# Evicting two neighbouring PSUM banks with one instruction, with the contracted weights kept by row tile

## The reference

```python
masked_w = weight * mask[None, :, :]
w_bot = jnp.einsum('bg,got->bot', y, masked_w)
out = x + jnp.einsum('bnt,bot->bno', x, w_bot) + bias
```

## Time and profile before

| | us |
|---|---|
| median of 3 runs | 600.57 (600.22 to 600.57) |
| span of the profiled execution, first to last instruction | 598.5 |
| TensorE matmul busy | 591.2 (99%) |
| TensorE weight load busy | 517.5 (86%) |
| VectorE busy | 318.5 (53%) |
| ScalarE busy | 138.5 (23%) |
| POOL busy | 38.0 (6%) |

### The profile page before, as it was taken

How to read it: one execution, slowest core, us unless ns; L and a number is a source line. 1 busy time by engine, 2 the same in 40 slices (tenths; PEclk the granted TensorE clock), 3 DMA queues, 4 the chain that set the end, 5 groups by cost and what they waited for, 6 DMA issues and landing times.

```text
span 598.5 us, 15121 instructions
## 1 busy us (share of the span) xinstructions
PE 591.2 (99%) x6460; PEld 517.5 (86%) x6460; DVE 318.5 (53%) x542; ACT 138.5 (23%) x278; POOL 38.0 (6%) x34
## 2 busy tenths in 40 slices
PE   7899999999999999999999999999999999999998
PEld 5899988888898888888888888888888888889887
DVE  5565445455465555555554554555555645545343
ACT  5343222122122122221221221221212212211000
POOL 3430000000000111111110000000000000000000
PEclk9999999999999999999999999999999999999999
DMA  9987556776667798998987777586775767767842
GB/s 320 406 299 221 184 179 247 230 231 245 213 220 248 254 312 274 328 334 263 319 304 243 246 228 240 207 263 207 252 225 204 278 207 229 248 213 259 298 147 88
DMA packets 62994, 148.35 MB, mean 248 GB/s; under 512 B 6976, under 2 KB 13504, under 8 KB 62928
## 3 DMA queue, kind: packets, MB, share of 16 engines
q1 hardware_dynamic: 41184, 113.00, 58.3%
q10 hardware_dynamic: 21744, 34.39, 15.4%
HBM read 113.81 MB, written 33.55 MB: 246 GB/s over the span
## 4 chain that ended last, share of the span: by engine, by line
PE 97%; DMA 1%; SPq 1%; POOL 0%; issue 0%; DVE 0%; POOLq 0%
PE ps L464 76%; PE ps L437 20%; DMA xs<-in_mask 1%; SPq L226 1%; PE ps L474 1%; SPq L232 0%; POOL wm L205 0%; PE ps L420 0%; DVE wbot L342 0%; DVE staged L375 0%; POOLq L203 0%
## 5 line engine op out<-in xcount | busy, mean ns | idle before, releaser
L464 PE MATMUL ps<-wbot,xs 128*128 128x256 f32 (+1 forms) x2272 | 456.6, 360 | 0.8 <-DVE wbot L342 0.8
L464 PEld LDWEIGHTS ps<-wbot,xs 128*128 128x128 f32 x2272 | 390.3, 190 | 51.9 <-issue 1.6
L282 ACT ACTIVATE wbot<-ps 128x512 f32<-128x512 f32 (+2 forms) x277 | 137.2, 568 | 400.6 <-PE ps L437 392.5
L370 DVE TENSOR_TENSOR staged<-ps,staged 128x512 f32<-128x512 f32 (+1 forms) x118 | 77.9, 660 | 226.6 <-PE ps L464 226.6
L342 DVE COPY wbot<-ps 128x512 f32<-128x512 f32 (+2 forms) x274 | 159.2, 644 | 10.8 <-PE ps L437 7.9
L437 PEld LDWEIGHTS ps<-y_sb,wm 32*128 32x128 f32 x4096 | 122.1, 187 | 21.3 <-issue 17.8
L437 PE MATMUL ps<-y_sb,wm 32*128 32x128 f32 x4096 | 134.5, 277 | 1.7 <-issue 1.0
L356 DVE TENSOR_TENSOR staged<-staged,bias_sb 128x512 f32<-128x512 f32 (+1 forms) x119 | 79.1, 664 | 0.0
L205 POOL TENSOR_TENSOR wm<-wm,mask_sb 128x512 f32<-128x512 f32 x16 | 20.9, 1327 | 245.4 <-DMA mask_sb<-in_mask 245.4
L370 DVE TENSOR_TENSOR staged<-ps,bias_sb 128x256 f32<-128x256 f32 (+1 forms) x24 | 12.3, 514 | 34.0 <-PE ps L464 32.3
L205 POOL TENSOR_TENSOR wm<-wm,xs 128x512 f32<-128x512 f32 x13 | 16.4, 1272 | 22.1 <-DMA xs<-in_mask 21.9
(11 more groups left out here) (4 smaller groups left out, 0.4 us busy)
## 6 DMA issues: line engine op xcount, KB each, us to landing
xs<-in_x SPq DMA_DIRECT2D x128, 512.0 KB, 4.2
out<-staged ACTq DMA_DIRECT2D x112, 256.0 KB, 4.4
staged<-in_xn SPq DMA_DIRECT2D x105, 256.0 KB, 3.7
wm<-in_w SPq DMA_DIRECT2D x12, 512.0 KB, 7.7
mask_sb<-in_mask SPq DMA_DIRECT2D x8, 512.0 KB, 7.9
out<-staged ACTq DMA_DIRECT2D x31, 128.0 KB, 3.7
wm<-in_w SPq DMA_DIRECT2D x8, 256.0 KB, 5.6
xs<-in_mask SPq DMA_DIRECT2D x4, 512.0 KB, 13.5
```

Of the source, the lines that this page charges most:

```text
L282: eng.activation(tile_place(b, j, first, end), tile_sums(b, j, first, end), ACT.Copy).then_inc(s_ev_a, 1)
L370: eng.tensor_tensor(at, by_batch(total), at if m >= OWN_X else bias_of(m), ALU.add).then_inc(s_o, 1)
L464: ins = eng.matmul(bank[:, h * width:(h + 1) * width], group[:, h, k, :], at, start=(k == 0), stop=(k == KT - 1))
```

## The change

ScalarE evicts row tiles 0 and 1 of a burst with one instruction over two neighbouring banks, and VectorE evicts tiles 2 and 3 with another, in all bursts. So that a pair lies in neighbouring banks, an even one first, `share_banks` plans the banks: a pair of a burst takes the even-aligned pair of banks whose later use is the oldest, a piece takes the single bank used longest ago; `TAKEN_FROM` says whose bank each takes, and `room` waits for that one. The 8 PSUM tensors are one tensor `ps`. The layout of `wbot` within a chunk and group was (k, h, 16 features) and is (row tile j, k, h, 4 features): a pair's values are regular in it, and a piece's moving operand, 16 features for one k and h, now lies in runs of 4 values where it had runs of 16. A burst has 2 parts, or 4 where it is cut, in `parts_of`; the test of the length of `parts_of(b)` against TILES in `group_ready` is left as it was.

```diff
-TAKEN = [(_b, _j) for _b in range(HALF) for _j in range(TILES)]
-for _m in range(LAST + 1):
-    TAKEN += [(_b, _j) for _b in bursts_before(_m) for _j in range(TILES)] + [(_m, None)]
-TAKEN += [(LAST + _i, None) for _i in range(1, len(ENDING))]
-BANK_OF = {_key: _i for _i, _key in enumerate(TAKEN)}
+BANK_OF, TAKEN_FROM = {}, {}
+def share_banks():
+    owner, given = {}, dict.fromkeys(range(BANKS), -1)
+    def take(key, bank, at):
+        BANK_OF[key], TAKEN_FROM[key], owner[bank], given[bank] = bank, owner.get(bank), key, at
+    def take_burst(b, at):
+        for p in range(2):
+            first = min(range(0, BANKS, 2), key=lambda i: (max(given[i], given[i + 1]), i))
+            for j in (0, 1):
+                take((b, 2 * p + j), first + j, at)
+    def take_piece(i, at):
+        take((i, None), min(range(BANKS), key=lambda n: (given[n], n)), at)
+    clock = 0
+    for b in range(HALF):
+        take_burst(b, clock := clock + 1)
+    for m in range(LAST + 1):
+        for b in bursts_before(m):
+            take_burst(b, clock := clock + 1)
+        take_piece(m, clock := clock + 1)
...
-def on_vector(b, j):
-    return j == 3 or j == 1 and b not in BY_VECTOR[:2]
+def on_vector(b, p):
+    return p == 1
...
 def parts_of(b):
     if b == HALF - 2:
-        return tuple((b, j, 0, SOON if j else GROUPS) for j in range(TILES))
+        return tuple((b, p, 0, SOON if p else GROUPS) for p in range(2))
     if b == HALF - 1:
-        return (tuple((b, j, 0, SOON) for j in range(TILES)) +
-                tuple((b - 1, j, SOON, GROUPS) for j in range(1, TILES)) +
-                tuple((b, j, SOON, GROUPS) for j in range(TILES)))
+        return (tuple((b, p, 0, SOON) for p in range(2)) + ((b - 1, 1, SOON, GROUPS),) +
+                tuple((b, p, SOON, GROUPS) for p in range(2)))
     if b % CS < CS - 1:
-        return tuple((b, j, 0, GROUPS) for j in range(TILES))
-    return tuple((b, j, at, end) for at, end in ((0, SOON), (SOON, GROUPS)) for j in range(TILES))
+        return tuple((b, p, 0, GROUPS) for p in range(2))
+    return tuple((b, p, at, end) for at, end in ((0, SOON), (SOON, GROUPS)) for p in range(2))
...
-        sums = wbot[:, :].rearrange("p (i q k h o) -> p i q k h o", i=CS, q=GROUPS, k=KT, h=GB)
+        sums = wbot[:, :].rearrange("p (i q j k h o) -> p i q j k h o", i=CS, q=GROUPS, j=TILES, k=KT, h=GB)
...
-        def tile_ready(eng, b, j):
-            eng.wait_ge(s_s1, b * TILES + j + 1)
+        def pair_ready(eng, b, p):
+            eng.wait_ge(s_s1, b * TILES + 2 * p + 2)
...
+        def pair_place(b, p, first, end):
+            at = sums[:, first:end, c, 2 * p:2 * p + 2, :, :, :] if u % 2 else sums[:, c, first:end, 2 * p:2 * p + 2, :, :, :]
+            return at.rearrange("p g j k h o -> p (j k h) g o")
+        def pair_sums(b, p, first, end):
+            at = BANK_OF[b, 2 * p] * BANK
+            return psum[:, at:at + 2 * BANK].rearrange("p (a g o) -> p a g o", g=GROUPS, o=TO)[:, :, first:end, :]
         def tile_evicted(eng, b, j, end):
-            eng.wait_ge(s_ev_v if on_vector(b, j) else s_ev_a, DONE[b, j, end])
+            p = j // 2
+            eng.wait_ge(s_ev_v if on_vector(b, p) else s_ev_a, DONE[b, p, end])
...
                 if g in (0, SOON):
                     b = u * CS + end - 1
                     soon = g == 0 and len(parts_of(b)) > TILES
-                    for j in range(TILES):
+                    for j in (0, 2):
                         tile_evicted(eng, b, j, SOON if soon else GROUPS)
...
-                        at = sums[:, g, c:end, k, h, :] if u % 2 else sums[:, c:end, g, k, h, :]
+                        at = sums[:, g, c:end, :, k, h, :] if u % 2 else sums[:, c:end, g, :, k, h, :]
```

## The result

The changed kernel takes 641.71 us (639.45 to 643.01, 4 runs) against 600.57 (600.22 to 600.82, 4 runs): the ratio is 1.068, 95% interval 1.066 to 1.070. Forecast was 635.2, with a range of 628 to 648. Run once more beside the experiments it took 641.01 us.

The account below looks back on a forecast made before the run. TensorE, without slack, bounds the kernel and would wait for later-freed banks: 22.1 + 6.6 + 1.4 + 2.0 + 2.5 = 34.6 us, on a 598.5 us span 633.1, plus 2.07 gives 635.2 us; range 628 to 648.

Parts of the forecast that it names:

- From an eviction's end to TensorE: Delay from ScalarE's eviction ending to the waiting weights' load beginning, read from the start of the trace: 0.05 us.
- Regular places: Steady part, 34 places where the piece waits for VectorE's pair behind the bias addition: 0.65 us each, 22.1 us.
- Places without the bias: 13 places where VectorE has no or a short bias addition before the copy: 0.51 us each, 6.6 us.
- The three early ones: Three early places where matmuls with the identity lengthen burst B: 0.47 us each, 1.4 us.
- ScalarE's places: 8 places where the piece takes the bank of ScalarE's pair: 0.25 us each, 2.0 us.
- POOL beside L356: Two places where POOL's mask multiplications lengthen add_bias_to_x, delaying VectorE's copy: 2.5 us, by phase 0 to 4.
- The start: Bursts 2 to 7 and the first piece: later-freed banks against fewer instructions, set to zero, -0.8 to +0.5 us.
- The wait for all of burst 15: Unit's second half piece waits for the whole last burst: hidden by the stall ahead, otherwise 0.1 us, 8 times.
- Cover holds: Rival: VectorE's pair ends within 0.57 us, no piece waits, 599.4 to 600.6 us; 3% faster, 4% same, together.
- The pair at 1.37: Rival: VectorE's pair instruction is no cheaper than two copies, 1.37 us; loss 43.8 us, time 644; 7%.
- Reading slower: Rival: TensorE reads its moving operand in runs of 4 slower: up to 14 us on top, 650; 6%.
- The clock: Rival: PE's idling drops its clock to 1.2 GHz for each piece m: over 800 us; 1%.

Follow-up runs that it names:

- the first tile alone and the test mended: Changed kernel, pieces on ScalarE's bank, ScalarE evicting tiles 0 and 1 of burst A by an instruction each, `group_ready` test mended to `len(pairs_of(b)) > 2`: 600.48 us, ratio 1.000.
- The kernel with the bias behind: Changed kernel with add_bias_to_x of the coming piece issued behind VectorE's evictions and not ahead of them: 637.16 us, ratio 1.061.
- the one with the test mended: Changed kernel with only the `group_ready` test mended, so a unit's second half piece waits for the last burst's first three groups alone: 641.04 us, beside 641.01 unmended.
- the kernel where the piece is on time: Changed kernel, pieces on ScalarE's bank by a planner key, ScalarE evicting tiles 0 and 1 of burst A by an instruction each, test unmended: 602.32 us, ratio 1.003.

## Why the prediction was right, and where its sizes were off

**The mechanism was right.** PE has no slack, the first bank after two bursts had a margin of 0.22 us, and the change takes it away. The waits confirm it, and so does each kernel that moves the moment at which the awaited bank comes free. The margin itself was read too wide: with the 0.11 us from an eviction's end to the weights' load (below), about 0.11 of the 0.22 us was slack, an estimate.

In a regular place, us after the bursts' start, and the kernel's time:

| the piece waits for | bank free | piece starts | time |
|---|---|---|---|
| ScalarE's first tile | 1.79 | 2.01 | 600.5 |
| VectorE's first tile (8 places on ScalarE's pair) | 2.07 | 2.21 | 613.6 |
| ScalarE's pair | 2.26 | 2.40 | 622.6 |
| ScalarE's second tile (52 places) | 2.27 | 2.42 | 620.3 |
| VectorE's pair (8 places on ScalarE's pair) | 2.60 | 2.74 | 641.7 |

The number of instructions plays no part: of the kernels with row 1's time, the one with the first tile alone and the test mended has 406 on VectorE, as many as the kernel of the last row.

**The sum, 34.6 us, measured 40.7 in the profiled execution** from the first pair of bursts to the end. By its terms, from the starts of bursts in the trace:

- Pair's duration, 1.217 and 1.023 us: measured 1.217 and 1.024 (from the earlier trace rows). Two banks in one instruction cost what the line through 96 and 512 elements says, and the bounds of 1.15 and 1.37 fall away.
- From an eviction's end to TensorE, 0.05 us: this was the term taken too small. 444.52 + 1.22 = 445.74, the weights' load begins at 445.85: 0.11 us. The row that I took it from the earlier trace rows was that of a row tile's load in the start, and not of a whole array's after row tiles; whether that makes the difference wasn't tried. The matmul then starts 0.03 after its load; that part comes back, as the 32 records of the two pieces take 0.03 less. So 0.06 us in each of 60 places, 3.6 us.
- Regular places: 0.65 forecast, 0.71 measured (9.82 - 9.11).
- Places without the bias: 0.51 forecast, 0.65 measured. Beside the 0.06, the copy started 1.32 us after the bursts and not 1.24: the wait for all four tiles instead of two, which the text left out. I had looked at the spread of the last four matmuls, 0.02 us, and not at that of their signals. 13 places, 1.1 us; ScalarE's part of it is 0.04 in 8 places. The three early ones are 0.61 for 0.47, likewise.
- ScalarE's places: 0.25 forecast, 0.37 measured in 7, none at m = 2, where burst 9 waits for its mask; 2.6 us for 2.0.
- POOL beside L356: 2.5 us forecast in two places, 1.2 of it above two ordinary waits; in the profiled execution three places are 0.64, 0.64 and 0.81 us above their like, 2.1 us. The kernel with the bias behind shows it: 641.4 - 637.2 = 4.2 us gone, of which 36 x 0.06 = 2.2 is the earlier copy, and most of the spread between runs with it. The forecast that this is a matter of phase, 0 to 4 us, holds: in the changed kernel's second trace (span 637.2) one place is 0.16 us above its like, in the one with the test mended (span 640.3) four are, by 2.9 us together. With the clock in the start (below), that is nearly all of the spread.

These differences, from unrounded starts, add up: 2.2 us in the 36 places with the bias, 1.9 in the 13 without, 0.4 in the early three, 0.6 in ScalarE's and 0.9 by POOL are 6.0, and 34.6 + 6.0 = 40.6. All five have the same sign; that the range held them is in part luck, since its upper end had 9 us for a dearer pair, which did not come.

**The start**, set to zero: in the profiled execution the first pair of bursts after the first piece begins 2.0 us later than before (24.93 for 22.91). In the kernels with pairs whose clock stayed at 1.00 it is between -0.1 and 0.6 (the forecast said -0.8 to 0.5), and the rest is the clock, below. The two runs that the median lies between have a mean clock of 1.000, so the 41.1 us between the medians hold no such part.

**Edits costed at nothing.** The layout: 600.34, right, by the kernel that has it alone. Banks of the bursts: the waits show none of L460 for L394; right. The wait for all of burst 15: hidden behind the late piece, as written (641.04 beside 641.01), and in the kernel where the piece is on time 1.8 us, where the text said 0.8: 0.17 in place of 0.1 us at the starts of 7 units and 0.13 before piece 8 is 1.3, and the remaining 0.5 us I can't place.

**Rivals.** Cover holds: decided at 0.57 us, the copy takes 1.217. The pair at 1.37: no. Reading slower: no. The clock: not in the steady part, 1.00 in each window of it, but see below. The change does what it says.

## What to carry to other kernels

When the bound engine runs without a gap, look for who frees its next buffer and by how much it is early; here 0.22 us in 600, at one place of a period, and it was all the kernel had. Merging two instructions saves their fixed part on an engine that may not need it, and holds the first half's buffer until the second is done: merge where nobody waits for the first half, which in this kernel was three of four pairs, and even there it gave nothing, since the engines that it relieved had slack. A planner that breaks ties by a buffer's number should break them by who is done first; in the kernel with pairs that line alone was worth 19 us.

## What the runs showed of the hardware

**Signals of row tiles come one after another.** The last matmuls of four row tiles end within 0.02 us, but an engine that waits for the first, second, third and fourth signal starts its eviction 1.19, 1.23, 1.28 and 1.32 us after the bursts' start: 0.043 us each. With signals on row tiles 1 and 3 alone the starts are 1.207 and 1.267. Both sets fit 0.025 us for each signal waited for and 0.017 for each row tile, an estimate from these six starts; so about 0.02 us between neighbours stays however few signals are raised.

**A clock that fell in the start in some executions and not in others.** In the profiled execution of the changed kernel PE waited 1.46 us for POOL's mask, and the granted clock was then 0.50, that is 1.2 GHz, for 3.4 us (its timeline, and its window in the columns of the earlier trace rows):

```profile
16.60 1.68 PE L460 MATMUL ps<-y_sb,wm 32*128 32x128 f32 x29 [1.46 <-POOL wm L229]
```

```profile
16.88:20.29 3.41, 3.41 (x71) 3.34 (x67) 0.36 (x1) 1.02 (x1) 0.00 (x0) 0.50 1.03 406
```

The second profile of the same kernel has the same pause and a full clock; the same records take 1.06 us and not 1.68:

```profile
16.24 1.06 PE L460 MATMUL ps<-y_sb,wm 32*128 32x128 f32 x29 [1.51 <-POOL wm L229]
```

```profile
14.00:20.00 6.00, 3.77 (x107) 3.59 (x100) 3.75 (x6) 3.57 (x5) 2.10 (x2) 1.00 1.02 404
```

The layout-alone kernel, which has no pair, showed such a fall too (1.53 us of pause, its profiled execution at 601.64 where the median is 600.34), so the change is not its cause. The kernel with the first tile alone and the test mended showed one at another place, at 8.5 us, behind a pause of 1.47 us. It is worth about 3.4/2 = 1.7 us where it happens, an estimate: the first pair of bursts behind the first piece begins at 24.93 us in the execution with the fall and at 22.94 in the one without. Of the 8 executions of the changed kernel the slowest two, 643.01 and 643.14, are the ones with a mean clock of 0.997; the others have 1.000. The prediction's sentence that a pause of 0.96 us leaves the clock alone stands; pauses of 1.5 us did in some executions and not in others, and what decides it these runs don't show. The waits of up to 1.5 us for a late copy in the steady part left it at 1.00.
